# A mixture-of-experts kernel: the shared experts' down products with weights and tokens exchanged

## What is computed

```python
x = x + attention(layernorm(x))            # 32 heads of 8, 8 key/value heads
xt = layernorm(x)                          # 2048 x 256
# routed: 2 of 8 experts a token, weighted by the normalized sigmoid scores
out = einsum('te,teh->th', comb, expert_out)
# shared: both experts (NSH = 2, I = 640) for every token
sgate = silu(einsum('th,jih->tji', xt, sg))
sup = einsum('th,jih->tji', xt, su)
out = out + einsum('tji,jhi->th', sgate * sup, sd)
x = x + out
```

## Time and profile before

| | us |
|---|---|
| runs | 959.50, 960.42, 963.53 (median 960.42) |
| the profiled execution | 959.4 |
| its span, first to last instruction | 957.7 |
| mean granted clock of TensorE | 0.977 |
| busy: TensorE matmul, its weight loads | 897.4, 570.2 |
| busy: ScalarE, VectorE, GpSimd | 592.1, 445.7, 275.3 |

### The profile page before, as it was taken

How to read it: one execution, slowest core, us unless ns; L and a number is a source line. 1 busy time by engine, 2 the same in 40 slices (tenths; PEclk the granted TensorE clock), 3 DMA queues, 4 the chain that set the end, 5 groups by cost and what they waited for, 6 DMA issues and landing times.

```text
span 957.7 us, 24218 instructions
## 1 busy us (share of the span) xinstructions
PE 897.4 (94%) x8205; PEld 570.2 (60%) x8206; DVE 445.7 (47%) x761; ACT 592.1 (62%) x736; POOL 275.3 (29%) x420
## 2 busy tenths in 40 slices
PE   6959999999999999999997999999999999999994
PEld 4523333333333333333346888888887888888883
DVE  5733334434443344444356767656653434334332
ACT  5769999999999999999982423342212222222221
POOL 4303333232333323333340000000012555444442
PEclk7979999999999999999997999999999999999998
DMA  4350555554444555532112207100027773565421
GB/s 139 105 174 35 179 206 203 196 191 167 148 167 157 205 205 202 196 95 88 31 50 71 66 1 253 38 8 23 1 75 264 259 210 90 160 165 142 143 38 22
DMA packets 41951, 123.67 MB, mean 129 GB/s; under 512 B 7608, under 2 KB 22968, under 8 KB 35760
## 3 DMA queue, kind: packets, MB, share of 16 engines
q1 hardware_dynamic: 30144, 109.37, 33.0%
q0 software_dynamic: 7008, 9.70, 5.7%
q10 hardware_dynamic: 4752, 4.01, 1.3%
HBM read 74.03 MB, written 49.02 MB: 128 GB/s over the span
## 4 chain that ended last, share of the span: by engine, by line
PE 75%; ACT 9%; DVE 6%; issue 5%; SPq 3%; DMA 1%; DVEq 0%; POOL 0%; POOLq 0%; ACTq 0%
PE ps L1618 17%; PE ps L1766 14%; PE ps L1571 13%; PE ps L1720 11%; ACT arena L920 7%; PE ps L1785 7%; PE ps L1733 5%; DVE ps L1118 3%; PE ps L1776 2%; PE ps L1671 1%; PE ps L1525 1%; SPq L529 1%; SPq L526 1%; PE ps L1747 1%; PE ps L1707 1%
## 5 line engine op out<-in xcount | busy, mean ns | idle before, releaser
L920 ACT ACTIVATE arena<-ps 128x1024 f32<-128x1024 f32 x336 | 317.0, 1044 | 5.3 <-PE ps L1571 5.3
L1618 PE MATMUL ps<-arena 128*32 128x256 f32 x4096 | 265.0, 385 | 0.1
L753 POOL TENSOR_SCALAR_AFFINE_SELECT arena<-arena 128x512 f32<-128x512 f32 x240 | 150.0, 638 | 302.0 <-ACT arena L931 202.4
L1571 PE MATMUL ps<-arena 64*128 64x512 bf16 (+1 forms) x1280 | 184.6, 342 | 20.6 <-SPq L568 6.2
L1618 PEld LDWEIGHTS ps<-arena 128*32 128x32 f32 x4096 | 111.8, 109 | 102.9 <-issue 38.2
L1118 DVE COPY_PREDICATED ps<-keep,ps 128x512 f32<-128x512 int32 (+1 forms) x128 | 80.5, 629 | 170.7 <-PE ps L1571 170.7
L1571 PEld LDWEIGHTS ps<-arena 64*128 64x128 bf16 x1280 | 53.6, 94 | 174.7 <-ACT arena L920 83.4
L1766 PE MATMUL ps<-wr_all,x2T 128*128 x648 | 145.7, 366 | 5.5 <-issue 3.5
L1766 PEld LDWEIGHTS ps<-wr_all,x2T 128*128 128x128 f32 x648 | 106.6, 190 | 27.6 <-issue 12.8
L1720 PE MATMUL ps<-x2T,wr_all 128*128 128x512 f32 x480 | 118.5, 398 | 1.2 <-issue 1.2
L931 ACT ACTIVATE arena<-ps 128x1024 f32<-128x1024 f32 x112 | 114.3, 1034 | 8.4 <-DVE ps L1118 3.6
(11 more groups left out here) (188 smaller groups left out, 731.6 us busy)
## 6 DMA issues: line engine op xcount, KB each, us to landing
w_scr<-wr_all SPq DMA_DIRECT2D x24, 1280.0 KB, 7.0
wr_all<-w_scr SPq DMA_DIRECT2D x24, 1280.0 KB, 5.7
raw<-w_experts SPq DMA_DIRECT2D x24, 640.0 KB, 7.1
arena<-q_scr SPq DMA_DIRECT2D x64, 64.0 KB
o_scr<-arena SPq DMA_DIRECT2D x128, 32.0 KB, 1.6
arena<-o_scr SPq DMA_DIRECT2D x16, 256.0 KB, 4.2
raw<-w_shared SPq DMA_DIRECT2D x6, 640.0 KB, 4.4
arena<-q_scr SPq DMA_DIRECT2D x32, 96.0 KB
```

Source lines behind the costliest of these rows:

```text
L753: nc.gpsimd.affine_select(out=dst, in_=src, compare_op=ALU.is_ge if own else ALU.is_gt, fill=0.0, base=0, pattern=[[0, REP], [-1 if own el ...
L920: nc.scalar.activation(prob[:, SLOT[unit(a, kt)], :, :].rearrange("p h q -> p (h q)"), score.rearrange("p b x -> p (b x)"), ACT.Exp, scale ...
L1571: return nc.tensor.matmul(ps[:, bank, :].rearrange("p (h q) -> p h q", h=2)[:, :, place * P:(place + tiles) * P], kst[r0:r0 + HALF, s, kt ...
L1618: last = nc.tensor.matmul(ps[32 * h:32 * h + 32, 6 + qc, a % 2 * QW:(a % 2 + 1) * QW], vst[:, s, kt, :], prob[:, SLOT[k], h, :], start=(no ...
```

## The change

The down product of a step is turned round. A 128x128 block of the down weights is loaded, and the hidden values of all 512 tokens of the chunk stream past it: 2 blocks x 3 = 6 matmuls of 512 columns (before: 12 of 256). The sums then have features on the partitions, one block of 128 features in each of the banks 4 and 5. They have to be turned back before they can be added to the rows:

- ScalarE, `turned_sums_out(c)`: copies both banks to `yT` in SBUF, after its ten steps of the chunk. `yT` lies partly where the attention's output was staged, so ScalarE first waits for the last stores of it (`o_stored`).
- TensorE, `turn_back(c)`: 8 transposes of 128x128 into banks 4 and 5, placed in the first step of the next chunk, behind up(0); for the last chunk behind `routed_up_first(0)`.
- VectorE, `add_shared(c)`: the four additions as before, now behind the split of the next chunk's first step, ahead of `ahead_of` and `routing`; for the last chunk after `xT_low(0, 0)` and ahead of `up(0, 0)`.

```diff
--- before.py
+++ after.py
@@ -338,6 +338,7 @@
         top[0] = HSH + HR * 2 * CT
         gsh = carve(2 * CT).rearrange("p (s t) -> p s t", s=2)
         hsf = carve(2 * CT).rearrange("p (s t) -> p s t", s=2)
+        yT = carve(KD * CT).rearrange("p (k t) -> p k t", k=KD)
         top[0] = ring_end
         wq_sb = carve(KD * D).rearrange("p (k n) -> p k n", k=KD)
         wk_sb = carve(KD * KV * HD).rearrange("p (k n) -> p k n", k=KD)
@@ -408,7 +409,8 @@
         w_loaded = [sem(f"w_loaded{n}") for n in range(WSLOTS)]
         c_xlo, s_hi, s_split, e_xlo, e_hThi, r_pos, r_pos_hot, r_place = (sem(n) for n in (
             "c_xlo", "s_hi", "s_split", "e_xlo", "e_hThi", "r_pos", "r_pos_hot", "r_place"))
-        s_gu, s_act, s_hid, s_down, s_out = (sem(n) for n in ("s_gu", "s_act", "s_hid", "s_down", "s_out"))
+        s_gu, s_act, s_hid, s_down, s_yT, s_back, s_out = (sem(n) for n in (
+            "s_gu", "s_act", "s_hid", "s_down", "s_yT", "s_back", "s_out"))
         e_in = [sem("e_in0"), sem("e_in1")]
         e_tx, e_xT, e_gu, e_act, e_hid, e_th, e_hT, e_mm, e_y = (sem(n) for n in (
             "e_tx", "e_xT", "e_gu", "e_act", "e_hid", "e_th", "e_hT", "e_mm", "e_y"))
@@ -954,10 +956,21 @@
                         act.wait_ge(c_lsb, NC + FIRST)
                         nc.scalar.activation(rt[:, 0, :, :], logits[:, :, :], ACT.Exp, scale=-1.0).then_inc(r_exp, 1)
 
+            def turned_sums_out(c):
+
+                act.wait_ge(s_back, c * 2)
+                for k in range(KD):
+                    act.wait_ge(s_down, c * KD + k + 1)
+                    nc.scalar.copy(yT[:, k, :], ps[:, 4 + k, :]).then_inc(s_yT, 1)
+
             root(NC + 1)
             x2_out(0)
-            for c in range(NC):
+            for qc in range(QC):
+                act.wait_ge(o_stored[qc], 16 * REP * NG + FIRST)
+            for c in range(NC - 1):
                 shared(c)
+                turned_sums_out(c)
+            shared(NC - 1)
 
             def xT_out(j, p):
                 act.wait_ge(e_tx, j + 1)
@@ -974,6 +987,7 @@
                     .then_inc(e_act, 1)
 
             xT_out(0, 0)
+            turned_sums_out(NC - 1)
             gate(0, 0)
             xT_out(1, 1)
 
@@ -1225,6 +1239,13 @@
                 for c in turned(step, 9):
                     logits_out(c)
 
+            def add_shared(c):
+
+                for t in range(TPC):
+                    dve.wait_ge(s_back, c * 2 + t // 2 + 1)
+                    nc.vector.tensor_tensor(x_rows(c, t), x_rows(c, t), ps[:, 4 + t // 2, t % 2 * D:(t % 2 + 1) * D],
+                                            ALU.add).then_inc(s_out, 1)
+
             def shared(c, between):
 
                 for q in range(STEPS):
@@ -1235,14 +1256,10 @@
                     dve.wait_ge(s_hi, step + 1)
                     nc.vector.tensor_tensor(hsh[:, q % HR, 1, :], hsf[:, q % 2, :], hsh[:, q % HR, 0, :].bitcast(F32),
                                             ALU.subtract).then_inc(s_split, 1)
+                    if c and q == 0:
+                        add_shared(c - 1)
                     ahead_of(step)
                     between(step)
-                if c == NC - 1:
-                    xT_low(0, 0)
-                dve.wait_ge(s_down, c + 1)
-                for t in range(TPC):
-                    nc.vector.tensor_tensor(x_rows(c, t), x_rows(c, t), ps[:, 4 + t // 2, t % 2 * D:(t % 2 + 1) * D],
-                                            ALU.add).then_inc(s_out, 1)
 
             merge_pair(NG - 1, 1)
             invert(0, 0)
@@ -1477,6 +1494,8 @@
             for c in range(NC):
                 shared(c, routing)
 
+            xT_low(0, 0)
+            add_shared(NC - 1)
             up(0, 0)
             xT_low(1, 1)
 
@@ -1726,16 +1745,24 @@
                 if q == 0:
                     pe.wait_ge(s_out, c * TPC + FIRST)
                 pe.wait_ge(s_split, c * STEPS + (q + 1))
-                o = (q % KI) * D
+                for k in range(KD):
+                    o = (q % KI) * D + k * P
+                    for w, v in UP_PRODUCTS:
+                        last = nc.tensor.matmul(ps[:, 4 + k, :], wr_all[:, q // KI, 2, w, o:o + P], hsh[:, q % HR, v, :],
+                                                start=(q == 0 and w + v == 0),
+                                                stop=(q == STEPS - 1 and (w, v) == UP_PRODUCTS[-1]))
+                    if q == STEPS - 1:
+                        last.then_inc(s_down, 1)
+
+            def turn_back(c):
+
+                pe.wait_ge(s_yT, (c + 1) * KD)
                 for t in range(TPC):
-
-                    for w, v in PRODUCTS:
-                        last = nc.tensor.matmul(ps[:, 4 + t // 2, t % 2 * D:(t % 2 + 1) * D],
-                                                hsh[:, q % HR, v, t * P:(t + 1) * P], wr_all[:, q // KI, 2, w, o:o + D],
-                                                start=(q == 0 and t % 2 == 0 and w + v == 0),
-                                                stop=(q == STEPS - 1 and (w, v) == PRODUCTS[-1]), skip_group_check=True)
-                if q == STEPS - 1:
-                    last.then_inc(s_down, 1)
+                    for k in range(KD):
+                        last = nc.tensor.transpose(ps[:, 4 + t // 2, t % 2 * D + k * P:t % 2 * D + (k + 1) * P],
+                                                   yT[:, k, t * P:(t + 1) * P], ident[:, :])
+                    if t % 2:
+                        last.then_inc(s_back, 1)
 
             project(0)
             transpose_rows(0)
@@ -1805,6 +1832,8 @@
                 for q in range(STEPS):
                     step = c * STEPS + q
                     shared_up(c, q)
+                    if c and q == 0:
+                        turn_back(c - 1)
                     if step == 0:
                         router(0)
                     for ahead in turned(step, 5):
@@ -1829,6 +1858,7 @@
                 shared(c)
             slot = slot_tile(0)
             routed_up_first(0, 0, slot, later=False)
+            turn_back(NC - 1)
             routed_up(0, slot, PIECES[1:]).then_inc(e_gu, 1)
             routed_xT(1, 1, 0)
             routed_up_first(1, 1, slot_tile(1))
```

## The result

The changed kernel takes 965.2 us (median of 12 runs, 963.9 to 971.11), the kernel before 962.6 (12 runs, 957.04 to 964.01). The ratio is 1.0054, 95% interval 1.0035 to 1.0073: slower by half a percent. The two medians alone would give 1.0027: the twelve times of the kernel before lie in two groups, five from 957.04 to 960.42 us and seven from 962.58 to 964.01, while none of the changed kernel's is under 963.9. The forecast was 0.24%, 962.7 us; the change cost about twice that, although the time lies in the range given. A step I gave a third of a chance came true and carries most of the loss.

A forecast was written before the change was run, and what follows sets the result against it. TensorE was taken to bound the shared experts. Down products -1.5, transposes back +2.4 and late additions +1.4 gave +2.3 us: 961.7 on the profiled execution, 962.7 on the median; range 960.0 to 966.0.

The forecast's parts named there:

- A step I gave a third of a chance: First slot product: the clock falls in TensorE's longer wait of 2.45 us; chances 0.20 short, 0.12 long.
- What a down product costs: Shared experts on TensorE: 6 matmuls in 1.375 us, 0.055 less a step; 28 steps' savings arrive, 1.5 us gained.
- Weight loads: Down product: 191 ns loads already hidden, halving them gives nothing further; the rival that they cost time, 930 us, chance 0.02.
- The transposes back: Chunk ends on TensorE: eight transposes take 0.79 us; three of four groups show on the chain, 2.4 us.
- the group of step 30: The transposes of chunk 2 on TensorE: disappear inside the longer wait before the first slot product.
- ScalarE's copies: Chunk ends: eight PSUM copies of 0.59 us each run behind TensorE's next up product and cost nothing.
- the row stores: Chunk 2's store lands about 674, needed at 684; chunk 3's begins at 728.13 behind an expert's load: no loads move.
- step 20: VectorE's product of step 21 comes some 1.2 us late, but TensorE needs it later, so no cost.
- The additions moved: VectorE from step 30: 1.41 us late at the one-hot table; TensorE's wait grows to 2.45 us, 1.4 us lost.
- a short one: Rival at the first slot product: a clock fall like that at 721.8 costs 1.6 us, giving 964.3; chance 0.20.
- a long one: Rival at the first slot product: a clock fall like that after 504 costs 3.8 us, giving 966.5; chance 0.12.
- The fall at 721.8: After the 1.85 us wait before 720.16: rival that this existing clock fall goes away, returning 1.6 us, 961.1; chance 0.12.

The follow-up runs named there:

- Experiment 3: Kernel before with only the additions moved, plus 30 idle transposes in TensorE's wait at the first slot product: 962.04 us, ratio 1.0037 against the kernel before.
- experiment 1: Changed kernel plus 25 idle transposes in TensorE's wait at the first slot product: 960.77 us, ratio 1.001 against the kernel before.
- experiment 10: Kernel before plus 16 idle transposes in its 1.67 us wait ahead of the first slot product: 959.35 us, ratio 0.9986.
- experiment 7: Kernel before with the first slot product one step later and 46 and 18 idle transposes in TensorE's two other long waits: 955.89 us, ratio 0.9932.
- 8: Kernel before with the turned down product alone, not turned back, first slot product one step later, two other long waits filled: 954.39 us, ratio 0.9924.
- 9: Changed kernel with the first slot product one step later and TensorE's two other long waits filled with idle transposes: 956.55 us, ratio 0.994 against the kernel before.
- experiment 2: Kernel before with only the four additions moved behind the split of the next chunk's first step: 964.36 us, ratio 1.0052.
- 5: Changed kernel with the first slot product one step later on TensorE (step 36 instead of 35): 958.61 us, ratio 0.9977 against the kernel before.
- 4: Kernel before with the turned down product alone, no copies or transposes back, additions unmoved, output wrong: 961.85 us, ratio 1.0015.
- 6: Kernel before with the first slot product one step later on TensorE, nothing else: 959.89 us, ratio 0.9983.

## Why the prediction was right and wrong

*What a down product costs.* Right in kind, too small in size. Six matmuls take 1.36 us (1.375 foretold). The up products beside them also went from 2.75 to 2.72, so a step takes 4.08 instead of 4.18 us: 0.10 saved, not 0.055. Under an even clock 2.57 us arrive, where I counted 1.5 in the kernel as it is. I had also said that the up products would stay at 2.75; they did not.

*Weight loads.* Right: the load of 191 ns stayed at 191 to 192 ns, half of the loads went, and nothing but the 2.57 us came of it. By the Trainium skill's rule ("TensorE: Matmul & The Clock Gate", "What overlaps and what doesn't") I had estimated some 30 us; the runs disagree.

*The transposes back.* 0.79 us each time by their own start to start, as foretold; in all 3.84 us for four groups, 0.96 each, where I had 0.79. A part of the rest lies in the up product behind them: at the end of chunk 0 it takes 2.82 us under the even clock instead of 2.72. What remains I did not part further. In the kernel as changed the group of step 30 was hidden in the wait, as I had it.

*ScalarE's copies, the row stores, step 20.* Cost nothing, as foretold: no wait on them, and up to chunk 3 there are only transposes less savings (+0.07 us, forecast +0.3).

*The additions moved.* Right: TensorE reached the first slot product 1.41 us later, and its wait is 2.51 us (2.45 foretold). Experiment 3 gives 1.42 for this step alone.

*The step that failed* is the one in which I gave this wait no price beyond its length. I set the fall of the clock beside the forecast as two rivals, 0.20 for a short one and 0.12 for a long one, reasoning that "the engine is full on both sides" and that the gap is half as long as the one at 504. It fell, and it fell long: 4.80 us, over the 3.8 I had named as the price of a long fall. The other terms of the sum held: 2.09 us in experiment 1, against the +2.3 of the forecast. With the fall the sum is 2.3 + 4.8 = 7.1 us; the five middle rows of the table give 6.91, and the start and the end, which varied by themselves, bring the spans to 5.6.

That the medians of 12 runs are only 2.6 us apart, close to my 2.3, is luck and no confirmation: my base of three runs had a median of 960.42, twelve gave 962.6, probably because the clock falls in a part of the runs of the kernel before too (experiment 10, not proved). From the median of its lower group of five, 959.5, to the changed kernel's it is 5.7 us. It is luck as well that the time lies in my range: the case that came true stood in the prediction at 966.5, outside the range, which ended at 966.0. I had the sign before me, a wait of 1.85 us followed by a fall while I was making one of 2.45, and still gave a fall of either length only 0.32.

*The fall at 721.8* I had priced at 1.6 us to the end. No profile shows that price: with or without a fall there, the time from tile 1's first piece to the end is the same (experiments 7 to 9).

*Ruled out:* that the clock fell because of transposes (experiments 1 and 2), that the turned product is slower (7 against 8), that the additions cost anything once no one waits for them (5 and 9: no idle time before the slot products).

## What to carry to other kernels

Price a wait on TensorE at its length and at a possible stretch of half clock behind it: in experiment 2, 1.4 us more of waiting cost 6.2. Ask also whether TensorE bounds the stage where the clock falls: behind the slot product the fall cost 4.8 us, behind tile 1's first piece nothing that reached the end. When work is moved on an engine that is not the bound, look for the stretch in which that engine has no idle time, and for who waits at its end. If such a wait grows, moving the waiting work one step later or filling the wait with idle transposes is cheap: in experiment 7 one number and 46 idle transposes at the start of the stage brought the 0.7%, by the stretches; the 18 at tile 1 brought nothing that can be seen.

## What was not expected of the hardware

How long a wait must be before the clock falls is no fixed number here. Waits of 1.97, 2.51 and 3.05 us before the first slot product were followed by a fall of 7 to 10 us; the one of 1.67 us was not in the profile. The wait of 1.85 us before tile 1's first piece is the same in nine profiles: in five of them a fall of some 3.4 us follows (before, after, and experiments 2, 4, 5), in four none (1, 3, 6, 10). The fall comes up to 1.5 us after work has resumed and goes on while the engine is full: 10.2 us after the wait of 2.51 us. So a small shift can decide over some microseconds, and this would put the times of such a kernel into groups, as those of the kernel before are. A difference below half a percent is better read from a stretch between two events of the traces than from medians.
